# Splitting the output weights on ScalarE and GpSimd in the last steps of attention, and starting the projection there

## What is computed

```python
x = x + attention(layernorm(x))     # 16 query heads, 4 key/value heads, head width 128
x = x + experts(layernorm(x))       # 32 experts and 32 empty ones, 8 chosen per token

# attention: q, k rotated, then elu + 1; running sums over the tokens
state = state + k[..., :, None] * v[..., None, :]
z = z + k
num = einsum('bhe,bhed->bhd', q, state)
den = einsum('bhe,bhe->bh', q, z)[..., None] + EPS
out = (num / den).reshape(bsz, seq_len, H * HD) @ Wo.T
```

## Time and profile before

| what | us |
|---|---|
| median of three runs | 966.79 (961.83 to 968.75) |
| the profiled execution, own time | 969.43 |
| its span, first to last instruction | 967.6 |

### The profile page before, as it was taken

The page is one execution under the profiler, slowest core; times in us unless marked ns, Lnnn a source line. Parts: engine busy times, 40 slices in busy tenths (PEclk is TensorE's granted clock), DMA queues, the critical chain, the costliest instruction groups (busy, mean ns, idle before and its releaser), DMA issues. The chain is left out here.

```text
span 967.6 us, 14529 instructions
## 1 busy us (share of the span) xinstructions
PE 904.2 (93%) x4362; PEld 731.9 (76%) x4362; DVE 772.5 (80%) x1843; ACT 503.4 (52%) x867; POOL 482.4 (50%) x395
## 2 busy tenths in 40 slices
PE   4789999999999999999988999999997799999995
PEld 3667888888888888888857888888875567777783
DVE  6968888888888898888887777777776598888882
ACT  5445545555545555455565323223322388787782
POOL 2457656677666676566650000000003458687862
PEclk9979999999999999999999999999998899999998
DMA  8001111111111111110275377444218589899952
GB/s 312 6 22 61 39 50 59 46 49 39 61 50 45 49 61 39 50 59 35 82 277 192 128 264 262 144 154 150 71 66 278 162 256 320 268 284 297 320 108 38
DMA packets 67368, 127.06 MB, mean 131 GB/s; under 512 B 12072, under 2 KB 14504, under 8 KB 65232
## 3 DMA queue, kind: packets, MB, share of 16 engines
q1 hardware_dynamic: 58144, 114.67, 34.3%
q0 software_dynamic: 9136, 11.31, 6.6%
HBM read 106.53 MB, written 32.90 MB: 144 GB/s over the span
## 5 line engine op out<-in xcount | busy, mean ns | idle before, releaser
L595 POOL TENSOR_TENSOR a_t<-a_t 128x512 f32<-128x512 f32 x80 | 105.1, 1314 | 102.8 <-DVE a_t L358 102.8
L604 POOL TENSOR_TENSOR a_fQ<-a_fQ,a_den 128x512 f32<-128x512 f32 x64 | 88.0, 1375 | 71.8 <-DVE a_den L396 71.8
L213 PE MATMUL a_PQ<-w_h,a_xT_h 128*128 128x512 f32 x384 | 107.9, 403 | 10.2 <-DVE w_l L345 9.6
L782 PE MATMUL r_PY<-w_h,r_o_h 128*128 128x512 f32 x256 | 105.8, 413 | 3.4 <-DVE r_o_l L884 3.4
L1070 POOL TENSOR_SCALAR r_vr<-r_mv 128x1 f32<-128x1 f32 x16 | 8.4, 526 | 196.6 <-DVE r_mv L895 196.6
L213 PE MATMUL a_PQ<-w_l,a_xT_h 128*128 128x512 f32 x384 | 105.3, 397 | 0.0
L1214 POOL DMA_INDIRECT m_xg<-xn2d,si x64 | 81.4, 1272 | 44.7 <-DVE m_xg L1343 17.4
L213 PE MATMUL a_PQ<-w_h,a_xT_l 128*128 128x512 f32 x384 | 103.5, 391 | 0.0
L782 PE MATMUL r_PY<-w_h,r_o_l 128*128 128x512 f32 x256 | 101.0, 395 | 0.0
L782 PE MATMUL r_PY<-w_l,r_o_h 128*128 128x512 f32 x256 | 100.5, 392 | 0.0
L392 DVE CUSTOM_DVE_ANT_0 a_m<-a_fQ,a_z 128x128 f32<-128x128 f32 x256 | 100.4, 445 | 0.0
(11 more groups left out here) (182 smaller groups left out, 2244.0 us busy)
## 6 DMA issues: line engine op xcount, KB each, us to landing
oT<-a_o SPq DMA_DIRECT2D x64, 256.0 KB, 2.4
v_l<-in_wgu SPq DMA_DIRECT2D x32, 512.0 KB
...
v_l<-oT SPq DMA_DIRECT2D x11, 1024.0 KB, 7.2
...
v_h<-oT SPq DMA_DIRECT2D x5, 1024.0 KB, 6.8
out<-r_x SPq DMA_DIRECT2D x18, 256.0 KB, 2.0
```

Source lines behind the costliest of these rows:

```text
L213: last = eng.matmul(bank[:, :], a[:, k, :], w[:, 4 * i + k, :], start=s == 0 and k == 0, stop=s == 2 and k == 3)
L595: eng.tensor_tensor(t1[:, r % 2, :], t1[:, r % 2, :], t2[:, r % 2, :], ALU.add).then_inc(sm["xr"], 1)
L604: eng.tensor_tensor(q, q, den[:, n % 2, :].unsqueeze(2).broadcast_to([P, 4, P]), ALU.mult).then_inc(sm["fs"], 1)
L782: last = eng.matmul(PY[c % 2][:, :], a[:, c % 2, h * P:(h + 1) * P], b[:, h, :], start=h == 0 and s == 0, stop=h == NH - 1 and s == 2)
```

## The change

Work is moved in five ways, and nothing is computed differently.

- SyncE loads the tiles of `Wo` one to three steps earlier (steps 60 to 62).
- ScalarE copies two of the tiles in every step from 61 on, behind `out(n-5)`, and in steps 65 to 68 one piece of chunk 0's rows each. All are done in attention.
- The low parts of tiles 0 to 10 go to GpSimd, one in each of steps 61 to 65 and two in each of 66 to 68, behind `a_low`. Those of tiles 11 to 15 stay on VectorE, at its end, behind a wait for GpSimd's eleventh. VectorE takes the low parts of the rows too, one in each of steps 65 to 68.
- TensorE makes the projection of chunk 0 for heads 0 to 3 between `attend(62)` and `attend(63)`, and for heads 4 to 7 behind the latter (`begin_o`). The PSUM bank `y0` is therefore shared by both blocks. Routing starts with heads 8 to 15.
- The load of chunk 3's rows waits for the projection of chunk 0, because those rows go to the memory in which chunk 0's low parts now lie.

```diff
@@ -87,7 +87,7 @@
-        PQ = [ps("PQ0"), ps("PQ1")]
+        PQ = [y0, ps("PQ1")]
         PT = [ps("PT0"), ps("PT1")]
@@ -182,12 +182,18 @@
+                    if n == NG - 4:
+                        eng.wait_ge(sm["pq"], unit_k(c) + 1)
+                        load_wo(0, 4)
+                        eng.wait_ge(sm["pq"], unit_q(n) + 1)
+                        load_wo(4, 8)
                     if n == NG - 3:
                         eng.wait_ge(sm["pq"], unit_q(n) + 1)
-                        load_wo(0, 12)
+                        load_wo(8, 12)
                     if n == NG - 2:
+                        eng.wait_ge(sm["pq"], unit_v(c) + 1)
+                        load_wo(12, 16)
                         eng.wait_ge(sm["pq"], unit_q(n) + 1)
-                        load_wo(12, 16)
                         load_o(0)
@@ -285,6 +291,19 @@
                     last.then_inc(sm["u"], 1)
+                def begin_o(heads_):
+                    if 0 in heads_:
+                        eng.wait_ge(sm["pqfree"], unit_q(NG - 2) + 1)
+                    for h in heads_:
+                        eng.wait_ge(sm["r_wol"], h + 1)
+                        eng.wait_ge(sm["r_ol"], h // 4 + 1)
+                        k, cols = h // 4, slice(h % 4 * P, (h % 4 + 1) * P)
+                        o_h, o_l = w_h[:, 20 + k, cols], w_l[:, 16 + k, cols]
+                        eng.matmul(PQ[0][:, :], o_h, w_h[:, h, :], start=h == 0, stop=False)
+                        eng.matmul(PQ[0][:, :], o_h, w_l[:, h, :], start=False, stop=False)
+                        eng.matmul(PQ[0][:, :], o_l, w_h[:, h, :], start=False, stop=False)
@@ -306,6 +325,10 @@
                         attend(n - 5)
+                    if n == NG + 3:
+                        begin_o(range(0, 4))
+                    if n == NG + 4:
+                        begin_o(range(4, 8))
                     if g == 1 and 1 <= c < NC:
@@ -421,6 +444,11 @@
                     eng.tensor_tensor(w_l[:, i, :], v_l[:, i, :], f(w_h[:, i, :]), ALU.subtract).then_inc(sm["r_wol"], 1)
+                def o_low(q):
+                    eng.wait_ge(sm["r_oh"], q + 1)
+                    eng.tensor_tensor(w_l[:, 16 + q, :], v_l[:, 16 + q, :], f(w_h[:, 20 + q, :]),
+                                      ALU.subtract).then_inc(sm["r_ol"], 1)
@@ -470,9 +498,11 @@
                         stats(c + 2)
-                    if n >= NG + 2:
-                        wo_low(2 * (n - NG - 2))
-                        wo_low(2 * (n - NG - 2) + 1)
+                    if n > NG:
+                        o_low(n - NG - 1)
+                eng.wait_ge(sm["r_wol"], 11)
+                for i in range(11, NH):
+                    wo_low(i)
@@ -543,6 +573,12 @@
                     copy(w_h[:, i, :], v_l[:, i, :], "r_woh")
+                def o_high(q):
+                    if q == 0:
+                        eng.wait_ge(sm["r_o0"], 16)
+                        eng.wait_ge(sm["pq"], unit_q(NG - 1) + 1)
+                    copy(w_h[:, 20 + q, :], v_l[:, 16 + q, :], "r_oh")
@@ -568,11 +604,13 @@
                         a_high(n - 4)
-                    if n >= NG + 2:
-                        wo_high(2 * (n - NG - 2))
-                        wo_high(2 * (n - NG - 2) + 1)
                     if 0 <= n - 5 < NG:
                         out(n - 5)
+                    if n >= NG - 3:
+                        wo_high(2 * (n - NG + 3))
+                        wo_high(2 * (n - NG + 3) + 1)
+                    if n > NG:
+                        o_high(n - NG - 1)
                     if g == 0 and c < NC:
@@ -598,6 +636,10 @@
+                def wo_low(i):
+                    eng.wait_ge(sm["r_woh"], i + 1)
+                    eng.tensor_tensor(w_l[:, i, :], v_l[:, i, :], f(w_h[:, i, :]), ALU.subtract).then_inc(sm["r_wol"], 1)
                 def scale(n):
@@ -622,13 +664,16 @@
                         a_low(n - 4)
+                    for i in {NG - 3: (0,), NG - 2: (1,), NG - 1: (2,), NG: (3,), NG + 1: (4,), NG + 2: (5, 6),
+                              NG + 3: (7, 8), NG + 4: (9, 10)}.get(n, ()):
+                        wo_low(i)
                     if g == 0 and c < NC:
...
-def routing(nc, sm, x, wo, wc, bias, consts, oT, xn2d, out, si, ring, wgu, wd, w_h_, w_l_, v_h, v_l):
+def routing(nc, sm, x, wo, wc, bias, consts, oT, xn2d, out, si, ring, wgu, wd, w_h_, w_l_, v_h, v_l, y0):
@@ -720,6 +765,8 @@
                 def load(c):
+                    if c == 3:
+                        eng.wait_ge(sm["r_y"], 1)
                     eng.wait_ge(sm["r_ol"], 4 * (c - 2))
@@ -779,7 +826,11 @@
                         for s, (a, b) in enumerate(steps):
-                            last = eng.matmul(PY[c % 2][:, :], a[:, c % 2, h * P:(h + 1) * P], b[:, h, :],
+                            rows = a[:, c % 2, h * P:(h + 1) * P]
+                            if c == 0:
+                                first = (w_h_[:, 20 + h // 4], w_h_[:, 20 + h // 4], w_l_[:, 16 + h // 4])[s]
+                                rows = first[:, h % 4 * P:(h % 4 + 1) * P]
+                            last = eng.matmul(PY[c % 2][:, :], rows, b[:, h, :],
                                               start=h == 0 and s == 0, stop=h == NH - 1 and s == 2)
@@ -832,7 +883,8 @@
-                for c in range(NC):
+                project(0, range(8, NH))
+                for c in range(1, NC):
                     project(c, range(0, 3))
@@ -872,10 +924,6 @@
-                def low(i):
-                    eng.wait_ge(sm["r_woh"], i + 1)
-                    eng.tensor_tensor(wo_l[:, i, :], v_l[:, i, :], f(wo_h[:, i, :]), ALU.subtract).then_inc(sm["r_wol"], 1)
@@ -957,24 +1005,14 @@
                 eng.memset(neg[:, :], -0.5).then_inc(sm["r_neg"], 1)
-                o_low(0, 0)
-                o_low(0, 1)
-                low(6)
-                low(7)
-                o_low(0, 2)
-                low(8)
-                low(9)
-                o_low(0, 3)
-                for i in range(10, NH):
-                    low(i)
+                for q in range(4):
+                    o_low(1, q)
                 eng.wait_ge(sm["r_cst"], 16)
...
                 eng.tensor_tensor(wc_r[:, :, 1, :], wc_s[:, :, :], f(wc_r[:, :, 0, :]), ALU.subtract).then_inc(sm["r_wcl"], 1)
-                for q in range(4):
-                    o_low(1, q)
                 for c in range(NC):
@@ -1027,18 +1060,9 @@
-                o_high(0, (0, 1))
-                high(6)
-                high(7)
-                o_high(0, (2,))
-                high(8)
-                high(9)
-                o_high(0, (3,))
-                for i in range(10, NH):
-                    high(i)
+                o_high(1)
                 eng.wait_ge(sm["r_wc"], 16)
                 copy(wc_r[:, :, 0, :], wc_s[:, :, :], "r_wch")
-                o_high(1)
                 for c in range(NC):
```

More of the change, by code:

```diff
@@ L42, in rows_of, with attention @@
     return v[:, i:i + 4, :].rearrange("p k (h t) -> p (k h) t", t=P)
-def attention(nc, sm, x, wq, wk, wv, wo, tabs, consts, oT, w_h, w_l, v_h, v_l):
+def attention(nc, sm, x, wq, wk, wv, wo, tabs, consts, oT, w_h, w_l, v_h, v_l, y0):
     with ExitStack() as ctx:
@@ L681, in routing @@
         id0 = sb("id0", [P, 64])
-        PY = [ps("PY0"), ps("PY1")]
+        PY = [y0, ps("PY1")]
         PX, PR, PK, PB, PW = ps("PX"), ps("PR"), ps("PK"), ps("PB"), ps("PW")
@@ L1462, in build @@
         ring7 = ring + [(v_h[:, 20:24, :], None, None, None)]
-        routing(nc, sm, x, wo, wc, bias, cr, oT, xn2d, out, si, ring7, wgu, wd, w_h, w_l, v_h, v_l)
+        routing(nc, sm, x, wo, wc, bias, cr, oT, xn2d, out, si, ring7, wgu, wd, w_h, w_l, v_h, v_l, y0)
+        shared.close()
         experts(nc, sm, wgu, wd, xn2d, out, si, ring, cr, w_h, w_l, v_h)
```

8 lines of the change are left out of this document (3 added, 5 removed).

## The result

The changed kernel takes 974.23 us (median of 6 runs, 972.70 to 975.57), the kernel before 966.44 us (6 runs, 961.83 to 968.75): ratio 1.0082, 95% interval 1.0051 to 1.0114. It is slower, by 7.8 us on the medians. The forecast was 971.9. Of the two profiled executions (975.57 and 969.43 us) the new one is 6.1 us longer, and its span 6.2 (973.8 against 967.6).

A forecast was written before the change was run, and what follows sets the result against it. TensorE is fully busy behind chunk 0's first projection, so its end decides: barrier 522.2, products to 527.8, clock 1.6, so 529.4 against 524.35; +5.1 on median 966.79 gives 971.9 us. Range 963 to 978 (8 in 10).

The forecast's parts named there:

- 24 products leave routing, 5.46 us: Routing's start: 24 of chunk 0's 48 products move into time in which TensorE waits for others, saving 5.46 us.
- GpSimd's tiles block the reduce, 3 x 1.1, step 62 hidden: Steps 62 to 65: each GpSimd weight tile blocks VectorE's reduce for 1.1 us; idle time hides step 62's; 3.3 us cost.
- ScalarE's copies: "nothing more": Attention's last steps: two copies a step (1.13 us a pair) delay ScalarE's exponentials, ending inside the blocked reduce; no added cost.
- the first rival: Weight tiles do not block VectorE's reduce; ScalarE's copies could hold back a step by up to 1.7; 967.3 us, chance 0.20.
- Pieces of rows ahead of `masked`, 2.3 + 0.5: Steps 65 and 66: VectorE's pieces of rows delay `masked(62)` by 2.3 us and `masked(63)` by 0.5 more.
- The end of the block: Attention's end: after `a_low(63)`, GpSimd's four tiles end at 518.7, VectorE's five at 521.8, barrier at 522.2 us.
- The clock, 1.6: TensorE's restart behind the barrier: a slow stretch costs 1.6 us, as before; ends 0 and 4.8 (all 24 products slow).
- `x` and the loads: 0: Loads of first tiles (step 61) and the first residual's `x`: no waiting, 0; upper ends 0.8 and 0.7 us.
- Behind it: From 524.35 to 718.5 us TensorE is always busy, so a shift of the first projection's end moves everything behind equally.

The follow-up runs named there:

- e5: Changed kernel with all 48 products back in routing, weight tiles left where the change put them; 978.86 us, ratio 1.0122 to the kernel before.
- e10: Kernel before plus one extra unread GpSimd subtraction behind `a_low` in each of steps 61 to 64; 963.88 us, ratio 1.0022 to the kernel before.
- e1: Changed kernel with GpSimd's first four weight tiles cleared by memset in place of the subtraction; 974.03 us, ratio 1.0056 to the kernel before.
- e3: Changed kernel with an own semaphore for VectorE's last five tiles, so they need not wait for GpSimd's eleventh; 972.19 us, ratio 1.0040 to the kernel before.
- e2: Changed kernel with VectorE's pieces of rows one step later, behind `masked`, and ScalarE's ahead of its weight tiles; 971.90 us, ratio 1.0037 to the kernel before.
- e4: Changed kernel with 20 more unread products behind head 7's, keeping TensorE at work until the barrier; 973.50 us, ratio 1.0060 to the kernel before.

## Why the prediction was right

The time at which chunk 0's products end was forecast as 529.4 and is 529.47, which is 529.7 in the old frame; the seam grew by 5.3 us where 5.1 were forecast. The forecast median, 971.9, lies 2.3 us below the measured 974.2, which is inside the range. Step by step:

- **24 products leave routing, 5.46 us.** Right: e5 gives 5.4, and that they hold nobody back.
- **GpSimd's tiles block the reduce, 3 x 1.1, step 62 hidden.** Right. Four long instructions appear; VectorE's idle time ahead of the rotation of step 62 shrinks from 1.40 to 0.63, and with 0.23 more ahead of its `a_V_l` hides the first; `masked(61)` is 3.2 us later; e10 finds three on the path, each as long as GpSimd's instruction makes it. The Trainium skill (SBUF — State Buffer, "Who interferes with whom") has the rule that two such instructions exclude each other and the first keeps the port. The traces agree: in e1 a memset, which reads nothing, leaves 0.28 us, and in e3, without the wait, the five tiles take 4.15 us in place of 3.10.
- **ScalarE's copies: "nothing more".** Right only beside the blocks. In e1, without them, 2.2 of 3.3 us stay: 1.3 are waits for `a_e`, for which the first rival allowed up to 1.7, and most of the rest is the hold by `scale`, which neither the forecast nor that rival had.
- **Pieces of rows ahead of `masked`, 2.3 + 0.5.** Right: e2 wins 2.7, and against before `masked(62)` comes 2.1 us later behind `masked(61)`, `masked(63)` 0.45 later behind `masked(62)`. `masked(63)` was forecast at 509.7 and is at 509.4 in the old frame.
- **The end of the block.** The chain is the forecast one, 0.8 us shorter: the barrier at 521.4 in the old frame, not 522.2. 0.3 of it is `masked(63)`, 0.4 GpSimd's four tiles with the pieces that slip in between (5.90 us), 0.1 the barrier itself. TensorE's first product follows 0.13 us behind the block's first instruction; the forecast let both start together.
- **The clock, 1.6.** That a slow stretch comes was right, its length was mis-sized: 12 slow products, not 8, cost 2.4. Its two ends (0 and 4.8) held it. This and the barrier's 0.8 cancel, by luck. With 6 slow products, which e1 has behind the same idling, the clock would have cost 1.0 us less, and the sum would have come out 0.7 us too high.
- **`x` and the loads: 0.** Right here: ScalarE waits for no tile in step 61. (By the diff only tiles 0 to 7 are loaded a step earlier; 8 to 15 stay in steps 61 and 62.) e4 shows the wait for `x` as soon as the clock's loss is gone.
- **Behind it.** The 5.3 us of the seam are still there at the start of the experts (+5.7), as the 100% of TensorE said. Up to the end another 0.7 comes up, with a granted clock of 0.83 from the experts' first product to 790 us against 0.87 before; no edit touches that stage, and why is open. The medians' 7.8 lies above the traces' 6.2; the median of the kernel before alone moved by 6.9 between comparisons.
